# Moving the agreement branch two steps ahead of the scan's end, and spreading the split of the third and second expert weights over three engines

## The reference

```
h = take(W.T, x)
def ssm(x, A, B, C):                 # a scan over the 512 positions
    s = tanh(s @ A.T + x_t @ B.T)    # state of width 128
    return states @ C.T
h1 = ssm(layernorm(h), A, B, C)
h = h + (sigmoid(h1 @ Wg.T + bg) * h1) @ Wo.T + bo
xf = layernorm(h)
idx = top_1(xf @ gate_w.T)           # softmax over one value: weight 1
y = (silu(xf @ w1[idx].T) * (xf @ w3[idx].T)) @ w2[idx].T
h = h + y + gelu(xf @ sw1.T) @ sw2.T
```

## Time and profile before

| what | us |
|---|---|
| three runs, median (lowest to highest) | 182.01 (180.23 to 183.34) |
| the profiled execution's own time | 182.58 |
| its span in the profile | 180.7 |
| busy: PE, DVE, ACT, POOL | 138.5, 127.2, 104.7, 84.1 |
| granted TensorE clock, mean | 0.971 |

### The profile page before, as it was taken

The page is one execution under the profiler, slowest core; times in us unless marked ns, Lnnn a source line. Parts: engine busy times, 40 slices in busy tenths (PEclk is TensorE's granted clock), DMA queues, the critical chain, the costliest instruction groups (busy, mean ns, idle before and its releaser), DMA issues.

```text
span 180.7 us, 3231 instructions
## 1 busy us (share of the span) xinstructions
PE 138.5 (77%) x997; PEld 99.7 (55%) x997; DVE 127.2 (70%) x365; ACT 104.7 (58%) x239; POOL 84.1 (47%) x77
## 2 busy tenths in 40 slices
PE   0105997788898888886799988899939989999720
PEld 0104864666675666675445878466726657666510
DVE  1245676927499995999779899488825778887730
ACT  2001444589989983587779993675532645655400
POOL 3768874900000000343100658552687787886580
PEclk9999999969999999999999999999996999999995
DMA  4564345899000000012200033410122443433331
GB/s 153 150 184 138 97 140 195 278 384 365 7 0 0 4 0 4 2 60 95 79 4 0 29 91 114 134 32 16 47 45 31 45 42 33 44 33 34 29 33 15
DMA packets 9955, 14.37 MB, mean 80 GB/s; under 512 B 1936, under 2 KB 4624, under 8 KB 9936
## 3 DMA queue, kind: packets, MB, share of 16 engines
q1 hardware_dynamic: 5904, 10.45, 16.9%
q0 software_dynamic: 4032, 3.67, 13.3%
HBM read 10.71 MB, written 3.41 MB: 78 GB/s over the span
## 4 chain that ended last, share of the span: by engine, by line
DMA 22%; PE 20%; POOL 18%; DVE 14%; ACT 12%; issue 10%; POOLq 1%; SPq 1%; DVEq 0%
DMA w_sb<-x_rows,row_in 7%; PE bank L655 6%; POOL w_sb L415 6%; POOL emb_rows L371 5%; DMA emb_rows<-emb,tok_sb 5%; POOL out L422 4%; PE bank L680 4%; DMA xblk<-x_rows,row_in 4%; ACT attn_out L725 4%; DMA w_sb<-w 3%; ACT states L702 3%; ACT w_hl L742 3%; PE bank L478 2%; PE bank L668 2%; DMA out<-w_sb,row_of 2%
## 5 line engine op out<-in xcount | busy, mean ns | idle before, releaser
L422 POOL DMA_INDIRECT out<-w_sb,row_of x20 | 31.3, 1564 | 9.1 <-DVE w_sb L1205 4.8
L478 PE MATMUL bank<-states,sq_sb 128*128 128x128 f32 x108 | 27.1, 335 | 6.0 <-ACT states L702 1.6
L655 PE MATMUL bank<-w_hl,xblk_t 128*128 x120 | 30.4, 391 | 1.0 <-issue 1.0
L403 POOL TENSOR_TENSOR rstd<-vareps,cst 128x2 f32<-128x2 f32 x8 | 5.7, 710 | 45.7 <-DVE vareps L853 45.7
L478 PEld LDWEIGHTS bank<-states,sq_sb 128*128 128x128 f32 x108 | 17.4, 202 | 14.2 <-ACT states L702 13.8
L812 ACT ACTIVATE w_sb<-bank,factor 128x512 f32<-128x512 f32 x20 | 13.8, 688 | 19.4 <-PE bank L655 19.3
L476 PE MATMUL bank<-x_in,sq_sb 128*128 128x128 f32 x108 | 23.3, 299 | 1.6 <-ACT x_in L695 1.5
L415 POOL DMA_INDIRECT w_sb<-x_rows,row_in x16 | 17.5, 1094 | 12.4 <-issue 6.3
L702 ACT ACTIVATE states<-bank 128x128 f32<-128x128 f32 x54 | 14.9, 276 | 12.2 <-PE bank L478 12.0
L680 PE MATMUL bank<-w_hl,w_sb 128*128 x160 | 16.6, 246 | 5.7 <-DVE w_sb L1205 5.7
L476 PEld LDWEIGHTS bank<-x_in,sq_sb 128*128 128x128 f32 x108 | 17.9, 207 | 2.8 <-ACT x_in L695 1.6
(11 more groups left out here) (160 smaller groups left out, 288.9 us busy)
## 6 DMA issues: line engine op xcount, KB each, us to landing
w_sb<-w SPq DMA_DIRECT2D x24, 256.0 KB, 6.4
x_rows<-norm SPq DMA_DIRECT2D x4, 256.0 KB, 2.4
out<-attn_out SPq DMA_DIRECT2D x4, 256.0 KB, 3.1
late<-places SPq DMA_DIRECT2D x1, 619.5 KB, 8.3
sw_sb<-sw SPq DMA_DIRECT2D x2, 256.0 KB, 3.0
cst<-consts SPq DMA_DIRECT2D x1, 420.0 KB, 3.3
sq_sb<-sq SPq DMA_DIRECT2D x1, 384.0 KB, 3.7
out<-w_sb,row_of POOLq DMA_INDIRECT x20, 3.3
```

What stands on the lines that cost most here:

```text
L422: pool.indirect_dma_start(out=out, out_offset=bass.IndirectOffsetOnAxis(ap=row_of[:, k:k + 1], axis=0), in_=out_blk[k % RING], in_offset=N ...
L478: pe.matmul(pre, at, states[:, i * COLS:(i + 1) * COLS], start=False, stop=True).then_inc(pre_ready, 1)
L655: mm = pe.matmul(hb[:], xblk_t[:, k % 3, b * P:(b + 1) * P], w[:, bass.ds(e * INNER + a * EXPERTS * INNER, INNER)], start=(j == 0), stop=( ...
```

## The change

The agreement's branch moves from behind step 52 to behind step 51 (`BRANCH_STEP`), so that steps 52 and 53 both come behind it. Gate 0 goes behind step 49 and pair 0's product with C behind step 50, into bank 6 (`c_bank`), where it is ahead of the branch; gate 1 stays ahead of the branch. If the states did not agree, pair 0's product would be made again; `agreed` tells DVE that this is settled. Of the split, ACT keeps 12 of 16 high halves (8 of w3, 4 of w2). DVE makes the other 4 of w2 in one instruction of 2048 columns, then 4 low halves of w3, the 4 low halves of its own in one instruction, and the last 4 of w2 one by one, all ahead of the agreement's chain. POOL makes the other 4 low halves of w3, each by two instructions: w * scale in place, then minus the high half; they stand ahead of its inverse roots.

```diff
+BRANCH_STEP = STEPS - 3
+POOL_LOWS = EXPERTS // 2
+OWN_HIGHS = EXPERTS // 2
...
+        c_bank = lambda n: bank[6 if n == 0 else n % 2]
...
+            for k, j in enumerate(range(EXPERTS - POOL_LOWS, EXPERTS)):
+                cols = slice(j * INNER, (j + 1) * INNER)
+                pool.wait_ge(w_high, j + 1)
+                pool.tensor_scalar(w3_sb[:, cols], w3_sb[:, cols], scale[:, W3:W3 + 1], None, ALU.mult).then_inc(w3_scaled, 1)
+                pool.wait_ge(w3_scaled, k + 1)
+                pool.tensor_tensor(w3_hl[:, 1, cols], w3_sb[:, cols], w3_hl[:, 0, cols], ALU.subtract).then_inc(w3_low_rest, 1)
             for n in range(PAIRS):
                 ts = slice(2 * n, 2 * n + 2)
                 pool.wait_ge(var2_ready, n + 1)
...
-            for i in range(STEPS - 1):
+            for i in range(BRANCH_STEP + 1):
                 advance(i)
...
-                if i == STEPS - 3:
+                if i == BRANCH_STEP - 2:
+                    pe.wait_ge(wgc_ready, 1)
+                    gate(0)
+                if i == BRANCH_STEP - 1:
+                    pe.matmul(c_bank(0)[:, 0:PC], ct, kept(0), start=True, stop=True).then_inc(c_done, 1)
+                if i == BRANCH_STEP:
                     pe.wait_ge(close_ready, 1)
                     pe.transpose(bank[7][0:1, 0:P], close_row[:, 0:1], ident).then_inc(close_turned, 1)
-                    pe.wait_ge(wgc_ready, 1)
-                    gate(0)
-                if i == STEPS - 2:
                     gate(1)
                     pe.wait_ge(agree_ready, 1)
                     ok = pe.value_load(agree_i[0:1, 0:1], min_val=0, max_val=1)
...
-
+            pe.sem_inc(agreed, 1)
+            for i in range(BRANCH_STEP + 1, STEPS - 1):
+                advance(i)
             pe.wait_ge(state_ready, STEPS)
...
-                if 0 <= j < 2 * EXPERTS:
+                if 0 <= j < 2 * EXPERTS - OWN_HIGHS:
...
-                if i == STEPS - 2:
+                if i == BRANCH_STEP:
                     act.wait_ge(bg_ready, 1)
                     gate(0)
                     gate(1)
...
-            for j in range(EXPERTS):
-                w3_low(j)
-            for j in range(EXPERTS - 3):
-                w2_low(j)
...
+            dve.tensor_scalar(w2_hl[:, own_chunks, 0, :], by_chunk(w2_sb[:, own_cols]), scale_of(W2), None, ALU.mult
+                              ).then_inc(own_high, 1)
...
+            for j in range(EXPERTS - POOL_LOWS):
+                ins = w3_low(j)
+            ins.then_inc(w_split, 1)
+            dve.wait_ge(own_high, 1)
+            w2_low(own.start, own.stop)
+            for j in range(own.start):
+                dve.wait_ge(w_high, EXPERTS + j + 1)
+                ins = w2_low(j, j + 1)
+            ins.then_inc(w_split, 1)
...
-            w2_low(EXPERTS - 3)
             dve.wait_ge(close_turned, 1)
             dve.tensor_reduce(agree_i[:], bank[7][0:1, 0:P], AX.X, ALU.min).then_inc(agree_ready, 1)
-            w2_low(EXPERTS - 2)
-            w2_low(EXPERTS - 1)
```

More of the change, by code:

```diff
@@ L276, in build @@
         seq_pre, seq_state, seq_kept = sem("seq_pre"), sem("seq_state"), sem("seq_kept")
-        seq_gate, seq_tanh = sem("seq_gate"), sem("seq_tanh")
+        seq_gate, seq_tanh, seq_c, agreed = sem("seq_gate"), sem("seq_tanh"), sem("seq_c"), sem("agreed")
+        w3_scaled, w3_low_rest, own_high = sem("w3_scaled"), sem("w3_low_rest"), sem("own_high")
         bg_ready, resid_ready = sem("bg_ready"), sem("resid_ready")
@@ L523, in _ @@
                     pe.matmul(gate_bank(n)[:, 0:PC], wgc[:], kept(n), start=True, stop=True).then_inc(seq_gate, 1)
+                pe.matmul(c_bank(0)[:, 0:PC], ct, kept(0), start=True, stop=True).then_inc(seq_c, 1)
+                pe.wait_ge(seq_c, 1)
                 pe.wait_ge(seq_tanh, 2)
+            pe.sem_inc(agreed, 1)
+            for i in range(BRANCH_STEP + 1, STEPS - 1):
+                advance(i)
             pe.wait_ge(state_ready, STEPS)
@@ L546, in _ @@
                         pe.wait_ge(sh_split, 3)
-                    if n >= 2:
+                    if n >= 3:
                         pe.wait_ge(gated_ready, n - 1)
-                    pe.matmul(bank[n % 2][:, 0:PC], ct, kept(n), start=True, stop=True).then_inc(c_done, 1)
+                    if n >= 1:
+                        pe.matmul(c_bank(n)[:, 0:PC], ct, kept(n), start=True, stop=True).then_inc(c_done, 1)
                 if 1 <= s and s + 1 < PAIRS:
@@ L633, in _ @@
             pe.wait_ge(w_split, 3)
+            pe.wait_ge(w3_low_rest, POOL_LOWS)
             pe.wait_ge(experts_ready, 1)
@@ L763, in _ @@
                     gate_tanh(n).then_inc(seq_tanh, 1)
-            advance(STEPS - 1)
+            for i in range(BRANCH_STEP + 1, STEPS):
+                advance(i)
             def gelu(n):
@@ L986, in _ @@
             w1_low(slice(3 * INNER, 8 * INNER)).then_inc(w_split, 1)
[L988 to L994, removed]
+            own = slice(EXPERTS - OWN_HIGHS, EXPERTS)
+            own_cols = slice(own.start * INNER, own.stop * INNER)
@@ L996, in w3_low @@
+            own_chunks = slice(own.start * IC, own.stop * IC)
+            by_chunk = lambda ap: ap.rearrange("i (c d) -> i c d", d=P)
+            dve.tensor_scalar(w2_hl[:, own_chunks, 0, :], by_chunk(w2_sb[:, own_cols]), scale_of(W2), None, ALU.mult
+                              ).then_inc(own_high, 1)
             def w3_low(j):
                 cols = slice(j * INNER, (j + 1) * INNER)
[L998 to L1003, removed]
@@ L1005, in _, with w2_low @@
-            for j in range(EXPERTS):
-                w3_low(j)
-            for j in range(EXPERTS - 3):
-                w2_low(j)
+                dve.wait_ge(w_high, j + 1)
+                return dve.scalar_tensor_tensor(out=w3_hl[:, 1, cols], in0=w3_sb[:, cols], scalar=scale_of(W3),
+                                                in1=w3_hl[:, 0, cols], op0=ALU.mult, op1=ALU.subtract)
+            def w2_low(first, end):
+                chunks = slice(first * IC, end * IC)
+                return dve.scalar_tensor_tensor(out=w2_hl[:, chunks, 1, :], in0=by_chunk(w2_sb[:, first * INNER:end * INNER]),
+                                                scalar=scale_of(W2), in1=w2_hl[:, chunks, 0, :],
+                                                op0=ALU.mult, op1=ALU.subtract)
@@ L1034, in _ @@
                     dve.wait_ge(c_done, n + 1)
+                    if n == 0:
+                        dve.wait_ge(agreed, 1)
                     if n >= 2:
```

4 lines of the change are left out of this document (2 added, 2 removed).

## The result

| | median (lowest to highest), us | ratio to the kernel before, 95% |
|---|---|---|
| before, in the same comparison | 181.15 (180.23 to 183.34) | |
| after | 190.56 (187.78 to 193.38) | 1.044 (1.025 to 1.064) |

The change makes the kernel slower by 4.4%, outside the range of the forecast.

What follows compares the result with a forecast made beforehand. Around the change the kernel was taken to go through one engine at a time (DVE, PE, then DVE and POOL). The profiled 182.58 plus a loss of 1.3 gave 183.9, or 183.3 us on the median's level; range 180.6 to 186.0.

Steps and rivals of the forecast that it cites:

- kept out until about 65.2: POOL's halves wait for DVE's first pause, behind `diff`, and delay the first inverse root: loss 1.3 us, chance 0.45.
- the second rival: POOL gets the port at each DVE instruction's end, then blocks DVE: agreement's chain 8.6 us later, net +8.0, chance 0.16.
- The cost from `agree_i`: Register load and branch on PE, from the end of `agree_i` to step 52's start: 0.8 us taken.
- one more step 0.86: The second scan step now behind the branch on PE adds 0.86 us before pair 1's product.
- the sum had 1.83: From step 52's start behind the branch to pair 1's product with C: 0.64, 0.86 and 0.33 us, in all 1.83.
- a gain of 0.6: Pair 1's product with C starts at 69.4 instead of 69.99 if no engine disturbs another: 0.6 us (0.2 to 1.0).
- above 1.4 for the load and branch nothing is gained: Bound on the branch's cost on PE: with load and branch above 1.4 us, the change gains nothing.
- The sum of 9.0: POOL's eight instructions for w3's low halves, 4 x (1.24 + 0.9) + 0.4 for hand-overs: 9.0 us (8.2 to 10.3).
- nearer the first because it reads half: POOL's one-input product of 512 columns, put between 0.71 and 1.24 us: 0.9 taken.
- ACT's pace: ACT's tanh in the scan's steps follows the last in 0.86 us; taking four high halves off ACT gains nothing.
- DVE's run, put at 8.74: DVE's split work ahead of the agreement takes 8.74 us, so the agreement's chain starts at 64.9, 0.35 earlier.
- POOL would hold the first root: POOL's work ends at 74.2, so the first inverse root behind it starts there or at 74.6, against 73.11 before.

Runs made afterwards that it cites:

- the branch alone: Kernel before with the branch, gate 0, pair 0's product and `agreed` as in the change, the split as before; ratio 1.007 (1.003 to 1.012).
- without POOL's halves: Changed kernel with POOL's four low halves of w3 left out and set to zero; ratio to the kernel before 1.005 (0.998 to 1.012).
- the two ratios: Changed kernel against the kernel before, 1.044 (1.025 to 1.064), and the same kernel unaltered, measured once more, 1.045 (1.035 to 1.055).

## Why the prediction was wrong

**The step that failed** is "So I expect POOL to be **kept out until about 65.2**". It carried the pattern of an indirect DMA's issue over to whole instructions. In the runs POOL gets in during DVE's run, three pairs of instructions ahead of `close_row`'s end, and DVE pays 3.9 us. It was the second rival, turns, to which 0.16 was given. Its price was wrong in turn: it charged eight turns with POOL's whole instructions (8.6 in all), where six fell ahead of `close_row`'s end, and a turn costs 0.43 or 0.9. The Trainium skill, SBUF — State Buffer, section Who interferes with whom, has the lock last for the whole instruction; the traces agree that the two exclude each other, and disagree on the length: clearly for the product, 0.43 of 1.57, and less for the difference, 0.9 of 1.15. That the time (190.56) came out by the number of that rival (190.0) is chance: the rest comes from two terms that had the wrong sign or were missing.

**The branch.** "The cost from `agree_i` lies between 0.4 and 1.2; I take 0.8": it is 1.3 to 1.4. The row of before had 1.21 in it, of which gate 1 was taken to hide a part; nothing hides it. And "one more step 0.86" is 1.08, since a wait that stood in the code behind the branch holds step 53's input product. The two steps took 2.12 in the branch alone (67.07 to 69.19), where the sum had 1.83. Instead of a gain of 0.6, pair 1's product comes 0.05 later without POOL's halves (A 4.34 for 4.29), and 0.6 later where DVE's split stays that of the kernel before too (4.88, ratio 1.007). The bound "above 1.4 for the load and branch nothing is gained" rested on the 1.83; with 2.12 it would have been 1.1, below what was measured.

**The clock** stands in no step of the prediction. Behind PE's wait it costs 1.07 up to pair 1's product (4.52 for 3.45) and 1.00 from there to the root, 2.1 of the 6.02 in the profiled run. Of the rest, 0.7 is the branch (3.45 for 2.72), and 3.2 is DVE's: POOL's 3.9, less 0.5 by which DVE's shorter run alone brings `diff` forward (0.93 ahead of the state product without POOL's halves, 0.45 before) and the 0.2 that `agree_i` gains as no low half stands in front of it.

**POOL's eight instructions.** The sum of 9.0 is 11.1 where nothing disturbs them: the difference is 1.15 for 1.24, but the product 1.57 for 0.9, beyond its bounds. The choice "nearer the first because it reads half" was wrong: a product with a scale per partition, one input and float32 out, is dearer on POOL than a subtraction of two tiles. The Trainium skill, GPSIMD Engine Reference, section 3.1, gives its 769 ns as the best case of a loop over 512 elements; the product measured here took twice that, and by the 769 ns the sum would have been smaller still.

**What was right.** ACT's pace is 0.86 to 0.88 in steps 48 to 51 with or without its four high halves, so taking them off gave nothing. DVE's run, put at 8.74, is 8.76 where POOL leaves it alone, and `diff` is then 0.9 ahead of the state product of step 51. Gate 0 and pair 0's product cost 0.02 a step. That POOL would hold the first root was wrong for the change (POOL is idle for 6.90 ahead of it), and right where POOL's work is made to begin at `close_row`; there the root starts 11.44 behind the state product, but the prediction's own sum of 9.0 would have put it some 2 us too early.

**What stays open.** The traces put 6.0 and 6.5 us ahead of the first root; the two ratios say some 8 (6.4 to 10.1 by the second). The 1.8 ahead of the change is a low clock in a part that was not edited, and the 0.9 behind the root lies within what C varies by. Why the clock falls behind the branch in some runs and not in others was not settled either.

## What to carry to other kernels

An engine that is idle is not a free one: work given to POOL beside a run of two-input instructions of DVE is paid for by DVE, here some 0.43 us for each input tile of 512 columns, and where DVE's run ends in a chain that others wait for, all of it lands on the path. Before work is moved to an idle engine, look at who shares its way to SBUF at that time, and at what stands behind it on the path: either way round, early or late, POOL's halves cost 2 to 4% here. Where a branch is moved ahead of work that it used to stand behind, count its whole distance, from the data to the first instruction behind it, as time in which that engine does nothing, and look for waits in the code that had been harmless only because of the old order.

## What the runs showed of the hardware that was not expected

POOL and DVE share SBUF by turns at the ends of DVE's instructions, and a turn of POOL's is shorter than its instruction: 0.43 of 1.57 (one input) and 0.9 of 1.15 (two). A one-input instruction of DVE, `close`, was held as well, 1.10 for 0.23, and a reduction beside POOL's product was not, 0.28. A one-input product with a scale per partition takes 1.57 on POOL for 512 columns, longer than a two-input subtraction at 1.15 or an addition at 1.24. A register load and branch on PE take 1.2 to 1.4 from the data to the first matmul behind them. And a filled wait (3.65 us of products of zeros) put the fall of the clock off, but did not prevent it.
